# Moving the product of far rows and edge values from VectorE to ScalarE in the weighted-sum stages of a graph kernel

## The reference, cut to what matters

```python
x = x + L0(relu(layernorm(x)), edges)            # attention layer, untouched here
h = relu(layernorm(x))
# L1: three layers, 25,000 edges (src = row, dst = col), 100,000 nodes of 64 floats
x_, out = h, h
for l in range(3):
    f1 = relu(x_[row] @ nb_W[l] + nb_b[l]); f2 = relu(x_[col] @ self_W[l] + self_b[l])
    hh = relu(concat([f1, f2]) @ att1_W[l] + att1_b[l])
    mask = clip(sigmoid(hh @ att2_W[l] + att2_b[l]) * 1.5 - 0.45, 0, 1)
    d = clip((segment_sum(mask, row) + 1e-6) ** -0.5, 0, 10)
    vals = mask * d[row] * d[col]
    x_ = segment_sum(vals[:, None] * x_[col], row)      # the stage that the change touches
    out = out + x_
return x + out
```

## Time and profile before

| | |
|---|---|
| median of 3 runs | 3198.88 us |
| the profiled execution | 3199.13 us, span 3197.3 us |
| weighted sums of layer 0 | 2008.6 to about 2164 us of the span |
| weighted sums of layer 1 | 2461.6 to about 2617 us |
| weighted sums of layer 2 | 2917.6 us to the end |
| busy over the span | DVE 2195.2 us (69%), POOL 1913.7 (60%), PE 1780.0 (56%), ACT 1068.3 (33%) |

### The profile page before, as it was taken

One profiled execution on the slowest core, in us unless ns is written; L12 is line 12 of the kernel. 1 busy time (PEld: TensorE's weight loads), 2 busy tenths in 40 slices (PEclk: granted clock), 3 DMA queues, 4 the chain that ended last, 5 costly groups with the idle time before them and its releaser, 6 DMA issues.

```text
span 3197.3 us, 34323 instructions
## 1 busy us (share of the span) xinstructions
PE 1780.0 (56%) x8972; PEld 1443.3 (45%) x8972; DVE 2195.2 (69%) x5951; ACT 1068.3 (33%) x2292; POOL 1913.7 (60%) x1844
## 2 busy tenths in 40 slices
PE   1124444441399986653665654665665656655663
PEld 0023333331299975542454433453444544544442
DVE  6748888887877744434555553897866988766775
ACT  0024444442144420001333323553444644443221
POOL 0057777777888017776777775017773017773776
PEclk9975555565555555556777776897888987787555
DMA  0023332231122212214222211233332333333543
GB/s 7 3 54 82 84 88 82 83 86 41 41 86 86 83 60 69 71 50 96 62 63 61 64 40 34 70 85 96 98 104 64 88 88 94 102 98 84 126 119 85
DMA packets 283933, 238.03 MB, mean 74 GB/s; under 512 B 161125, under 2 KB 207611, under 8 KB 283637
## 3 DMA queue, kind: packets, MB, share of 16 engines
q1 hardware_dynamic: 226933, 196.13, 21.4%
q0 software_dynamic: 56832, 40.05, 5.5%
HBM read 163.62 MB, written 84.20 MB: 78 GB/s over the span
## 4 chain that ended last, share of the span: by engine, by line
POOL 48%; issue 18%; DVE 13%; PE 12%; DVEq 4%; DMA 2%; SPq 1%; ACT 1%; POOLq 0%; ACTq 0%
POOL big L1003 13%; POOL G L994 12%; POOL regs L1845 7%; POOL out L1010 6%; POOL regs L1854 5%; PE bank L923 5%; POOL x_after_layer L647 5%; DVE den L1271 3%; PE bank L916 3%; DVE big L1285 2%; DVE big L1591 2%; PE bank L872 1%; DVEq L1590 1%; PE bank L1451 1%; DVEq L1273 1%
## 5 line engine op out<-in xcount | busy, mean ns | idle before, releaser
L1003 POOL DMA_INDIRECT big<-layer_rows,late x392 | 425.9, 1087 | 305.8 <-SPq L1075 186.9
L1845 POOL DMA_INDIRECT regs<-in_x,G x200 | 213.8, 1069 | 234.8 <-DVEq L1711 174.1
L1451 PE MATMUL bank<-regs,SQ 99*128 99x256 bf16 x1764 | 274.8, 319 | 84.2 <-ACT SQ L1357 77.7
L647 POOL DMA_INDIRECT x_after_layer<-G,idx_s x200 | 197.0, 985 | 198.0 <-DVEq L808 135.9
L1870 POOL DMA_INDIRECT farf<-dst_float,VAL x196 | 252.8, 1290 | 59.7 <-issue 59.7
L1451 PEld LDWEIGHTS bank<-regs,SQ 99*128 99x128 bf16 x1764 | 189.3, 112 | 152.8 <-ACT SQ L1357 102.7
L1010 POOL DMA_INDIRECT out<-G,scat_i x196 | 194.7, 993 | 104.4 <-issue 61.4
L1854 POOL DMA_INDIRECT regs<-in_x,G x200 | 211.2, 1056 | 70.2 <-issue 59.7
L1271 DVE SCALAR_TENSOR_TENSOR den<-steps,late,bank 128x256 f32<-128x256 f32 x588 | 245.2, 472 | 9.6 <-PE bank L1451 9.3
L994 POOL DMA_INDIRECT G<-x_after_layer,own_i x196 | 200.6, 1023 | 69.2 <-issue 61.0
L994 POOL DMA_INDIRECT G<-x_after_layer,far_i x196 | 198.5, 1013 | 66.5 <-issue 66.5
(11 more groups left out here) (416 smaller groups left out, 5745.7 us busy)
## 6 DMA issues: line engine op xcount, KB each, us to landing
regs<-x_after_layer SPq DMA_DIRECT2D x96, 256.0 KB, 3.2
out<-regs SPq DMA_DIRECT2D x96, 256.0 KB, 2.1
XC<-row_of_far_degree SPq DMA_DIRECT2D x147, 128.0 KB, 3.4
den<-in_x SPq DMA_DIRECT2D x50, 256.0 KB, 2.7
x_after_layer<-den SPq DMA_DIRECT2D x50, 256.0 KB, 2.0
regs<-tile_nodes SPq DMA_DIRECT2D x50, 256.0 KB, 3.2
layer_rows<-TS SPq DMA_DIRECT2D x98, 128.0 KB, 2.0
regs<-in_x SPq DMA_DIRECT2D x46, 256.0 KB, 2.8
```

What stands on the lines that cost most here:

```text
L647: g.indirect_dma_start(x1_d, bass.IndirectOffsetOnAxis(ap=idx_s[:, b, k:k + 1], axis=0), G[:, b, k, 0, :], None, bounds_check=top, oob_is_ ...
L1003: ahead(g, l, REVERSED, lambda u, l=l: g.indirect_dma_start(far[:, tile_of(u // C, u % C), :], None, xt_d[l - 1], bass.IndirectOffsetOnAxi ...
L1451: ins = pe.matmul(bank[2 + 2 * b + k // 2][:, (k % 2) * 256:(k % 2) * 256 + 256], OH[b][0:RB1 + 1, k * P:(k + 1) * P], TAB[0:RB1 + 1, part ...
L1845: g.indirect_dma_start(GR[:, c % DEEP, k, 0, :], None, a["x"], bass.IndirectOffsetOnAxis(ap=own0[:, c * C + k:c * C + k + 1], axis=0), bou ...
```

## The change

DVE's `select` ends with `VAL1`; the product is made on ACT, as four copies of 128x64 with a scale that is read per partition from a column of `VAL1`. ACT does this for chunk i - 1 in step i, between `hot` and `rows`. `scan` and `turn_back` move one step later on their engines (lag 2 to 3, and 3 to 4), and with them `final` (3 to 4) and `rows` (4 to 5). SP's lists aren't touched: `store` stays at lag 5, `load` at lag 2.

```diff
@@ select(c), DVE
                 v.tensor_tensor(VAL1[:, C * c:C * c + C], DCc[:, C * c:C * c + C], VAL0[:, C * c:C * c + C], ALU.mult).then_inc(signal("o_val"), 1)
-                if c >= 2:
-                    v.wait_ge(signal("z_t"), l * NC1 + c - 1)
-                v.drain()
-                v.tensor_tensor(by_pair(Z[b]), by_pair(far[:, C * c:C * c + C, :]), bc(VAL1[:, C * c:C * c + C].rearrange("p (h q) -> p q h", h=2), F), ALU.mult).then_inc(signal("z_done"), 1)
@@ end of aggregate_dve
-            staged(NC1, [(0, select), (2, scan)] + ([(3, final)] if l == 2 else []))
+            staged(NC1, [(0, select), (3, scan)] + ([(4, final)] if l == 2 else []))
@@ L1_act
-                staged(NC1, [(0, hot)] + ([(4, rows)] if l < 2 else []))
+
+                def product(c, l=l):
+                    b = c % 2
+                    s_.wait_ge(signal("o_val"), l * NC1 + c + 1)
+                    if c >= 2:
+                        s_.wait_ge(signal("z_t"), l * NC1 + c - 1)
+                    for k in range(C):
+                        u = C * c + 2 * (k % 2) + k // 2
+                        ins = s_.activation(Z[b][:, k, :], far[:, C * c + k, :], ACT.Copy, scale=VAL1[:, u:u + 1])
+                    ins.then_inc(signal("z_done"), 1)
+                staged(NC1, [(0, hot), (1, product)] + ([(5, rows)] if l < 2 else []))
@@ L1_pe
-                staged(NC1, [(0, bring), (2, turn_z), (3, turn_back)])
+                staged(NC1, [(0, bring), (2, turn_z), (4, turn_back)])
```

## The result

The changed kernel takes 3600.23 us (3597.14 to 3600.62, 4 runs) against 3198.49 us: 1.1248 times, with a 95% interval of 1.1234 to 1.1262. The profiled execution took 3600.01 us with a span of 3598.2. 3572 was predicted, with a range of 3500 to 3640.

What follows compares the result with a forecast made beforehand. DVE's 3.00 us a step was taken to bound layers 0 and 1, POOL's scatters layer 2. New loops over SP add 156.0 + 156.2 + 61 = +373 to 3199.13: 3572 us, range 3500 to 3640.

Steps and rivals of the forecast that it cites:

- The loop in layers 0 and 1: SP's store, spread, landing, hot, product, rows: spans one step instead of two, 6.54 us against 3.00; +156.0 and +156.2 us.
- the 0.9: Layers 0 and 1: estimated us for the product on ACT, four activations of 128x64; bounds 0.5 and 1.6.
- the landing: Layers 0 and 1: from SP issuing spread, the copy of ids, to hot beginning on ACT, put at 3.38 us.
- Start and end of the stages: Layers 0 and 1: rows(0) ends 20.0 us after the first bring; the tail is put at no change.
- The tail: Layers 0 and 1: from the last hot to the last rows, 9.4 us before, put at no change.
- the loop over `load`: Layer 2: final, load, spread, hot, bring, select span two steps instead of three, 13.0 us a turn, 22 turns; +61 us.
- The sign given for it: Layer 2: scatters on POOL would come in bursts of four with gaps of a little over 1 us.
- DVE as the bound, faster: Rival, 3%: DVE's step decides, each of 98 steps gains 0.45 us, about 3163 us; needs SP's loop under 3.0.
- Only the stores close a loop: Rival, 6%: layer 2 stays with POOL because loads find their final early enough; +317, 3516 us.
- The copy did not land sooner: Rival, 7%: with emptier queues the copy of ids lands in 2.1 us, the step is 5.26; 3437 us.
- The 2.3 us: Landing of the copy of ids by the skill's fixed cost of about 2.0 us plus bytes over bandwidth.
- Activations like `hot`: Rival, 4%: activations with a scale per partition cost 0.72 us each, four 2.9, +2.0 for 84 steps; 3740 us.

Runs made afterwards that it cites:

- the run with only layer 2 mended: Changed kernel with SP's load at lag 3 instead of 2 in layer 2, store still at 5: 3529.34 us, 1.105 times the kernel before.
- The loop without a product: Kernel before with SP's store at lag 4 instead of 5 in layers 0 and 1, product still on DVE: 3427.66 us, 1.0737 times.
- the two last versions: Changed kernel with product at lag 2, store 8, load 4: 0.9889; kernel before with product on POOL in layers 0 and 1, store 7: 0.9858.
- the run with the store at lag 7: Changed kernel with SP's store at lag 7 instead of 5 and load at 3 instead of 2: 3233.28 us, 1.0121 times the kernel before.
- The fastest version: Kernel before with the product on POOL in layers 0 and 1, later scan, turn_back and rows, store at 7: 3148.75 us, 0.9858 times.

## Why the prediction was right

- *The loop in layers 0 and 1* is the mechanism. It is shown from both sides: made in the kernel before by one number (+235 us), and opened in the changed kernel by two (from 1.1248 to 1.0121).
- *Its size* was 6.54 and is 6.77 us. The product is near its estimate: one copy takes 0.333 us and the four span 1.05 us, from just before the end of `hot`, so 0.95 to 1.0 for the 0.9. The figures of the Trainium skill, "ScalarE: Activation LUTs", section "What ACT_TABLE_LOAD costs", give 0.333 us for 64 columns with one operand per partition, and this trace agrees. `hot`, product and `rows` together take 2.73 us, where 2.71 was summed. The term that was mis-sized is the landing, 3.38, and it has 0.21 of the 0.23 us: measured from SP's issue to the `hot` that waited for it, it has a median of 3.55 in layer 0 and a mean of 3.59. I had taken the median (3.4) and two single rows; in the kernel before the mean of the same distance was 3.50 in layer 0, with single ones up to 4.3. When every transfer lies in the chain, the chain pays the mean. So half of the 0.2 was in the trace already. The other half seems to belong to the chip or the execution and not to the loop: in the run with only layer 2 mended, where layers 0 and 1 run the same code, the mean is 3.47 and 3.49, the step 6.67 and the stage 319.5 us. The loop without a product had 3.42 and 3.46.
- *Start and end of the stages*: `rows(0)` ended 20.4 us after the first `bring` (20.0 predicted). The tail from the last `hot` to the next stage took 13.1 us instead of 11.5: the last `rows` now come quickly one after another, and each waits for the store two before it to land. I had put that at nothing. Of the 11.8 us that layer 0 missed, the longer step has 9.9 (the landing 9.0 of them), the tail 1.6 and the start 0.4.
- *Layer 2*: turns of 13.16 for 13.0, +65.6 for +61. The landing has 3.5 of the 4.6 that were missed (3.52 us in the mean for 3.36, in 22 turns), and the start 1.0: the first scatter came 21.3 us after the first `bring`, not 20.3. That it is the loop over `load` is shown by the run with only that list moved: 285.1 us. The sign given for it was not right in its form: not every four scatters stand apart by a little over 1 us, but every eight by about 3, since two chunks go round together.
- *The rivals*: DVE as the bound, faster, is what the two last versions reach (138 and 131 us), and there its condition holds: the loop over SP is spread over three steps, about 2.3 us or less for each. "Only the stores close a loop" failed in layer 2. The copy did not land sooner once the stage moved less: DMA in layer 0 fell from 83 to 38 GB/s, and the landing got a little longer. The Trainium skill, "DMA: Bandwidth & Descriptors", section "Latency and other measured facts", says that a lighter load of the HBM makes the fixed cost smaller; between these two loads no run here shows it. The 2.3 us that the prediction worked out from that page's fixed cost, which is fitted to DMAs that GpSimd issues, were not met by these copies of SP's, the fastest of which landed after 2.8 us. What did shorten the landing was its distance from the store, to 3.00 us with the store at lag 7, and the loop has no room for that, since the copy is asked for directly behind the store. DVE was busy for 120 us of 310, less than half, as the prediction said. Busy us and instructions of PE, PEld, DVE, ACT and POOL over most of the stages of layers 0 and 1 after (the last three numbers are granted clock, DMA share, GB/s):

```profile
2007.00:2317.00 310.00, 165.54 (x756) 116.14 (x756) 120.17 (x478) 123.87 (x325) 14.63 (x47) 0.54 0.17 38
2628.00:2940.00 312.00, 166.83 (x767) 117.50 (x768) 120.44 (x479) 125.23 (x330) 0.00 (x0) 0.58 0.17 38
```

- *"Activations like `hot`"* is out by the 333 ns.

## What to carry to other kernels

Where lags are written by hand, a step that is moved on one engine changes its distance to every list that waits for it, also on an engine whose list isn't touched: here SP issues an old chunk's store ahead of a new chunk's load, and the load inherits the store's wait. Add up the way round through such a pair once and divide it by the steps that it spans, before and after the move; as long as the quotient is under the bound it costs nothing (2.85 under 3.00), and one step later it is everything. And whoever moves work off the bounding engine moves the lists of the queues with it: the same idea gave 12.5% more time with SP's lists left alone, 1.2% more with them moved, and 1.1% less only once the product, too, stood a step later behind the select that it waits for. A load also costs more where it stands directly behind a store: 3.4 to 3.5 us and not 3.0 in this case.

## What the runs showed of the hardware

TensorE's granted clock was 0.95 over layer 0 before and 0.54 after, near the lower of its two levels (1.2 and 2.4 GHz), with `bring` at 2.74 us instead of 1.48. Ahead of its `bring`s PE had waited 4.5 us in 140 before, and 137.9 us in 300 after, always for `hot`; that this is why the clock fell was not tested. The groups of `bring` in layer 0 before (2010 to 2150) and after (2010 to 2310):

```profile
L1451 PE MATMUL bank<-regs,SQ 99*128 99x256 bf16 x561 | 74.2, 285 | 4.5 <-ACT SQ L1357 3.2 <-DVE VAL L1274 1.0
...
L1457 PE MATMUL bank<-regs,SQ 99*128 99x256 bf16 x551 | 122.7, 411 | 137.9 <-ACT SQ L1353 137.9
```

In the loop of layers 0 and 1 `bring` lies off the path. In the run with the store at lag 7 it lies on it: `bring` took 1.50 us in one turn and 2.51 in the next. There the granted clock was 0.84 over layer 0 and 0.93 over layer 1, and layer 0 took 11 us longer (177.3 and 166.4). `bring` has 38.5 us of 120 in the chain of waits of layer 0 and 29.5 of 120 in that of layer 1, which is most of the difference. The fastest version kept 0.99 in layer 0:

```profile
2002.00:2122.00 120.00, 93.14 (x756) 74.25 (x755) 113.43 (x472) 79.76 (x137) 40.31 (x93) 0.99 0.40 98
```

POOL's elementwise product of 128x256 f32 took 0.612 us beside a busy DVE, against 0.426 on DVE, and DVE's picks did not slow down for it: 0.472 us each in layer 0, 0.470 before.
